# A rotary rotation split between VectorE and GpSimd, in a kernel of attention and experts

## What is computed

```
q, k, v = x @ Wq.T, x @ Wk.T, x @ Wv.T          # 32 heads of 8 features
q, k = rope(q), rope(k)                         # the rotation
kmean = mean of k over chunks of 32 tokens
gate  = q . kmean, future chunks masked, own chunk forced
allowed = 4 best chunks of each query, and causal
p = softmax(q . k / sqrt(8)) over what is allowed;  o = p @ v
o = o * rsqrt(mean(o*o) + 1e-6) * weight * sigmoid(x @ Wg1.T @ Wg2.T)
x1 = layernorm(x + o @ Wo.T)
ffn = x1 + 2 shared experts(x1) + 4 of 16 routed experts(x1), weighted
y  = layernorm(x1 + ffn)
```

```
def _rope(t):
    t1, t2 = (t[..., :D // 2], t[..., D // 2:])
    return jnp.concatenate([t1 * cos - t2 * sin, t1 * sin + t2 * cos], axis=-1)
```

## Time and profile before

| | us |
|---|---|
| median of 3 runs | 1645.65 |
| lowest, highest | 1645.09, 1646.04 |
| profiled execution, its own time | 1644.96 |
| its span | 1643.2 |
| TensorE busy | 1470.5 |
| VectorE busy | 1249.4 |
| ScalarE busy | 825.3 |
| GpSimd busy | 543.9 |

### The profile page before, as it was taken

The page is one execution under the profiler, slowest core; times in us unless marked ns, Lnnn a source line. Parts: engine busy times, 40 slices in busy tenths (PEclk is TensorE's granted clock), DMA queues, the critical chain, the costliest instruction groups (busy, mean ns, idle before and its releaser), DMA issues.

```text
span 1643.2 us, 30121 instructions
## 1 busy us (share of the span) xinstructions
PE 1470.5 (89%) x11488; PEld 789.5 (48%) x11488; DVE 1249.4 (76%) x3115; ACT 825.3 (50%) x1066; POOL 543.9 (33%) x638
## 2 busy tenths in 40 slices
PE   4688899898998989988999989989899889998597
PEld 3323465435654455534655256543565346552354
DVE  6994779768796788967787787977889677886434
ACT  4309362573627554393634836266452845349121
POOL 3204332253223532244322532234422443225032
PEclk8758899998999989998999989999899998999799
DMA  6000000000000000000000000000000000000000
GB/s 232 1 0 2 27 1 1 1 27 14 2 1 14 14 14 2 1 14 27 2 1 1 27 14 1 1 14 15 14 1 1 14 14 2 1 1 27 1 1 13
DMA packets 15623, 22.96 MB, mean 14 GB/s; under 512 B 812, under 2 KB 12758, under 8 KB 15224
## 3 DMA queue, kind: packets, MB, share of 16 engines
q1 hardware_dynamic: 15480, 21.05, 4.0%
HBM read 16.86 MB, written 4.19 MB: 13 GB/s over the span
## 4 chain that ended last, share of the span: by engine, by line
PE 66%; DVE 16%; ACT 7%; DVEq 4%; issue 3%; DMA 1%; POOL 1%; SPq 0%; POOLq 0%; ACTq 0%
PE PS L488 17%; PE PS L471 16%; PE PS L625 6%; PE PS L404 6%; ACT UQ L854 4%; PE PS L374 3%; PE PS L479 3%; PE PS L421 3%; PE PS L395 2%; DVEq L992 2%; PE PS L635 2%; DVE CM L1183 2%; ACT UK L854 1%; DMA qET<-in_w 1%; DVEq L1085 1%
## 5 line engine op out<-in xcount | busy, mean ns | idle before, releaser
L904 POOL TENSOR_TENSOR hp<-hr,hp 128x512 f16<-128x512 f32 (+1 forms) x200 | 235.3, 1177 | 673.4 <-ACT hp L741 632.2
L1183 DVE TENSOR_REDUCE CM<-PS 128x32 f32<-128x1024 f32 x320 | 385.2, 1222 | 40.5 <-PE PS L404 34.7
L488 PE MATMUL PS<-W,hp 128*128 128x256 f16 (+1 forms) x2400 | 311.5, 274 | 12.6 <-POOL hp L904 12.6
L471 PE MATMUL PS<-x1T,W 128*128 128x512 f16 (+1 forms) x1200 | 315.5, 392 | 0.8 <-ACT hr L732 0.8
L732 ACT ACTIVATE hr<-PS,CF 128x512 f32<-128x512 f32 (+1 forms) x200 | 137.5, 687 | 284.3 <-PE PS L479 255.1
L488 PEld LDWEIGHTS PS<-W,hp 128*128 128x128 f16 (+1 forms) x2400 | 215.1, 98 | 83.4 <-issue 44.3
L999 DVE TENSOR_TENSOR hr<-hr,PS 128x512 f32<-128x512 f32 x176 | 120.1, 682 | 101.3 <-ACT hr L732 98.1
L741 ACT ACTIVATE hp<-hr 128x512 f16<-128x512 f32 (+1 forms) x178 | 113.1, 635 | 162.2 <-DVE hr L999 160.6
L471 PEld LDWEIGHTS PS<-x1T,W 128*128 128x128 f16 (+1 forms) x1200 | 110.2, 100 | 113.2 <-issue 31.6
L854 ACT ACTIVATE UK<-PS 128x1024 f32<-128x1024 f32 x160 | 152.6, 1035 | 11.8 <-PE PS L421 10.8
L854 ACT ACTIVATE UQ<-PS 128x1024 f32<-128x1024 f32 x160 | 151.6, 1043 | 2.7 <-PE PS L421 0.9
(11 more groups left out here) (143 smaller groups left out, 2082.6 us busy)
## 6 DMA issues: line engine op xcount, KB each, us to landing
xT<-in_xT SPq DMA_DIRECT2D x8, 512.0 KB, 3.8
v<-in_x SPq DMA_DIRECT2D x8, 512.0 KB, 3.8
out<-x1n SPq DMA_DIRECT2D x8, 512.0 KB, 2.9
qET<-in_w SPq DMA_DIRECT2D x1, 1664.0 KB, 21.6
UK<-in_w SPq DMA_DIRECT2D x1, 1584.0 KB, 8.7
UQ<-in_w SPq DMA_DIRECT2D x1, 1584.0 KB, 11.9
kz<-in_w SPq DMA_DIRECT2D x1, 1536.0 KB, 19.8
WA<-in_wa SPq DMA_DIRECT2D x1, 776.0 KB, 5.2
```

The lines of the kernel that those rows point to most:

```text
L471: mm = pe.matmul(PS[0:w, BK_H, :], W1[:, a, k, bass.ds(f0, w)], x1T[:, e, k, :], start=(n == 0), stop=(n == 5))
L488: mm = pe.matmul(PS[:, BK_Y + j // 2, (j % 2) * D:(j % 2 + 1) * D], hp[0:w, slot, a, j * P:(j + 1) * P], W2[0:w, e, bass.ds(c, 1), :].rear ...
L904: nc.gpsimd.tensor_tensor(hp[0:w, slot, 1, :], hr[0:w, slot, :], hp[0:w, slot, 0, :], ALU.subtract).then_inc(pool_hp, 1)
L1183: nc.vector.tensor_reduce(dst, src, AX.X, ALU.max).then_inc(dve_cm, 1)
```

## The change

VectorE keeps the two products of each tile, without drains, and counts a new semaphore `dve_rot` with each. The product with the sines goes to one of two buffers `ropew`, by j % 2; before it overwrites a buffer, VectorE waits for the tile two back to be done (`pool_rope`). GpSimd does the subtraction and the addition in `turn_halves`, drains and counts `pool_rope`. TensorE and ScalarE wait for `pool_rope` where they waited for `dve_rope`. In GpSimd's order tiles 0 and 1 of the next sequence stand at the end of the turn (those of sequence 0 at the start of turn 0), tile 2 in front of the stack work of tile 0, and tile 3 in front of that of tile 1.

```
+        ropew = sb("ropew", [P, 2, 2 * D])
...
-                pe.wait_ge(dve_rope, b * NT + 2)
+                pe.wait_ge(pool_rope, b * NT + 2)
...
-                pe.wait_ge(dve_rope, (b + 1) * NT)
+                pe.wait_ge(pool_rope, (b + 1) * NT)
...
-                    act.wait_ge(dve_rope, b * NT + j + 1)
+                    act.wait_ge(pool_rope, b * NT + j + 1)
...
+            def turn_halves(b, j):
+
+                pool.wait_ge(dve_rot, 2 * (b * NT + j) + 2)
+                o = rot[:, j, :].rearrange("p (h u f) -> p h u f", h=2 * H, u=2)
+                w = ropew[:, j % 2, :].rearrange("p (h u f) -> p h u f", h=2 * H, u=2)
+                nc.gpsimd.tensor_tensor(o[:, :, 0, :], o[:, :, 0, :], w[:, :, 1, :], ALU.subtract)
+                nc.gpsimd.tensor_tensor(o[:, :, 1, :], o[:, :, 1, :], w[:, :, 0, :], ALU.add)
+                pool.drain()
+                pool.sem_inc(pool_rope, 1)
+
+            def turn(b, m, more):
+
+                if b == 0:
+                    turn_halves(0, 0)
+                    turn_halves(0, 1)
                 settled_wait(pool, pe_pv, b * NG + 2)
                 nc.gpsimd.memset(EQ[:, :, :, CR:HW].bitcast(F32), 0.0)
                 nc.gpsimd.memset(EK[:, :, :, CR + NCH:HW].bitcast(F32), 0.0)
                 for j in range(NT):
 
+                    if j < 2:
+                        turn_halves(b, j + 2)
                     nc.gpsimd.tensor_scalar(EK[:, j, :, CR:CR + NCH], ind[:, j:j + 1, :].to_broadcast([P, H, NCH]),
                                             1.0, 0.0, ALU.mult, ALU.add)
...
                 causal(NG - 1, 1)
-
-            turn(0, None)
+                if more:
+                    turn_halves(b + 1, 0)
+                    turn_halves(b + 1, 1)
...
                     dve.wait_ge(pe_proj, b * NT + j + 1)
+                    if b * NT + j >= 2:
+                        dve.wait_ge(pool_rope, b * NT + j - 1)
...
-                    w = ropeb[:, :].rearrange("p (h u f) -> p h u f", h=2 * H, u=2)
+                    w = ropew[:, j % 2, :].rearrange("p (h u f) -> p h u f", h=2 * H, u=2)
...
-                    nc.vector.tensor_tensor(w, t, sj, ALU.mult)
-                    link(nc.vector.tensor_tensor(o, t, cj, ALU.mult))
-                    nc.vector.tensor_tensor(o[:, :, 0, :], o[:, :, 0, :], w[:, :, 1, :], ALU.subtract)
-                    nc.vector.tensor_tensor(o[:, :, 1, :], o[:, :, 1, :], w[:, :, 0, :], ALU.add).then_inc(dve_rope, 1)
-                    dve.drain()
+                    nc.vector.tensor_tensor(w, t, sj, ALU.mult).then_inc(dve_rot, 1)
+                    nc.vector.tensor_tensor(o, t, cj, ALU.mult).then_inc(dve_rot, 1)
```

More of the change, by code:

```diff
@@ L199, in build @@
         pe_proj = sem("pe_proj")
-        dve_rope = sem("dve_rope")
+        dve_rot = sem("dve_rot")
+        pool_rope = sem("pool_rope")
         act_v = sem("act_v")
@@ L905, in low @@
                                         ALU.subtract).then_inc(pool_hp, 1)
-            def turn(b, m):
+            def turn_halves(b, j):
[10 more added lines that the diff above has]
+                    turn_halves(0, 1)
                 settled_wait(pool, pe_pv, b * NG + 2)
@@ L958, in turn @@
                 causal(NG - 1, 1)
-            turn(0, None)
+                if more:
+                    turn_halves(b + 1, 0)
+                    turn_halves(b + 1, 1)
+            turn(0, None, True)
             for b in range(1, B - 1):
-                turn(b, b - 1)
-            turn(B - 1, B - 2)
+                turn(b, b - 1, True)
+            turn(B - 1, B - 2, False)
             for c in range(NC):
```

## The result

| | us |
|---|---|
| changed kernel, median of 13 runs | 1657.84 |
| lowest, highest | 1650.77, 1661.81 |
| kernel before, median of the 13 runs beside them | 1648.44 |
| ratio, with its 95% interval | 1.0056 (1.0041 to 1.0071) |
| profiled execution, its own time and its span | 1661.81, 1659.2 |

The change costs 0.56%, 9.2 us of 1648.44, with an interval of 6.8 to 11.7. The kernel before stands at 1648.44 in these runs, against 1645.65 in the three runs that the forecast was made from, so the forecast of +12.6 is to be compared with +9.2. The profiled execution is the slowest of the 13, so its span is not compared with the one before; places within a seam are.

A forecast was written before the change was run, and what follows sets the result against it. TensorE was taken to bound the kernel, busy 89% of the span, so VectorE's savings count only where TensorE waits. Seven seams +9.6 and turn 0 +3 gave +12.6 us on 1645.65, so 1658; own range 1650 to 1666, chance 0.56.

The forecast's parts named there:

- The LayerNorm 0.85 us earlier: At each seam, VectorE's shorter tiles 0 and 1 let the second residual addition end at 1345.8 instead of 1346.64 us.
- The router 1.5 us earlier: At TensorE's second wait in the seam, for x1T: router starts near 1355.1 instead of 1356.60 us.
- Halves of 0.67 us: GpSimd's subtraction or addition of 256 f32 elements, from a line through 128 and 512 elements; 1.35 us per tile.
- The queue's order gives the gain back, +0.1 us at the chunk means: Tile 3's halves stand behind tile 0's stack on GpSimd, so chunk means wait until 1359.15 instead of 1359.06 us.
- behind 1360 us nothing adds to a gain: TensorE stays busy behind 1360 us, so nothing there absorbs a delay or adds to a gain.
- The routing's blocking, +1.4 us per seam: VectorE's L1052 and L1059 now meet busy GpSimd before the gate rows; bounds 0 to 2.3, seven seams sum to +9.6.
- One sign of being right: TensorE's wait before L449, the gate rows, would be over 1 us.
- Turn 0, +3 us: First gate instruction moves from 41.44 to about 47 us, +5.5; selection gets back some 2.5; bounds 1 and 6.
- Rival 1: In the routing, VectorE's two instructions meet gaps: +0.1 per seam, +1 to +3 in turn 0, 1647 to 1649; chance 0.19.
- rivals 2 and 3: GpSimd's halves: rival 2 takes 0.43 us without more blocking, 1641 us, chance 0.09; rival 3 takes 1.16 us.
- Rival 3: GpSimd's halves take 1.16 us: +2.0 at chunk means, +1.4 behind, +5 in turn 0, 1672; 0.16 together with rival 4.
- Rival 4: TensorE's fall to 1.2 GHz behind the seam's waits reaches some 3 us further: 1668 us; 0.16 together with rival 3.

The follow-up runs named there:

- e2: Changed kernel with, from turn 1 on, GpSimd's halves of tiles 2 and 3 behind the stacks of tiles 0 and 1; ratio to the kernel before 1.0076.
- e5: Changed kernel with only the halves of tiles 0 and 1 of sequences 1 to 7 on GpSimd, the rest on VectorE; ratio to before 1.0134.
- e7: Kernel before, no halves on GpSimd: VectorE makes tiles 0 and 1 as a pair, four products, one drain, four halves; ratio to before 1.0005.
- e1: Changed kernel with GpSimd doing tile 3's halves right behind tile 2's, ahead of all stack work; ratio to the kernel before 1.0039.
- e3: Changed kernel with only turn 0 undone: sequence 0's four tiles rotated wholly on VectorE with drains; ratio to the kernel before 1.0025.
- e4: Changed kernel with GpSimd waiting behind tile 3's halves for the routing's end, before low parts and the stacks of tiles 1 to 3; ratio to before 1.0165.
- e11: Kernel before with both tile pairs on VectorE; GpSimd waits for LayerNorm before tile 1's stack, for routing before first low part and tile 3's stack; ratio 0.9953.
- e12: e10 plus GpSimd waiting for the routing before tile 3's stack, with the first low part ahead of it; 1635.82 us, ratio to before 0.9938.
- e10: Changed kernel, sequence 0 on VectorE; GpSimd's order: clear stacks, halves 0 and 1, stack 0, halves 2 and 3, stacks 1 to 3; ratio to before 0.9971.

## Why the prediction was right, point by point

- **The LayerNorm 0.85 us earlier: right.** 3.35 to 2.51, 0.84. It left out a condition, that GpSimd keeps away from the LayerNorm (e2, e5, e7). In the changed kernel the very order that costs time at the chunk means fulfils it.
- **The router 1.5 us earlier: right.** In the earlier trace rows it starts 1356.60 - 1348.34 = 8.26 us behind the rank rows, after the change 1366.62 - 1359.63 = 6.99 in this seam and 6.67 to 7.03 in all.
- **Halves of 0.67 us: slightly small.** 0.72 by the median; a drain and a count add 0.18 between tiles.
- **The queue's order gives the gain back, +0.1 us at the chunk means: right.** 11.01 to 11.08. e1 shows the cause: with the order changed they come at 9.34. But the sentence that behind 1360 us nothing adds to a gain was wrong: e1's gate rows come 1.03 us earlier than before the change, and the wait for the first low part takes it back.
- **The routing's blocking, +1.4 us per seam: the mis-sized term.** From the start of the chunk means to the end of the routing it was 1366.91 - 1359.06 = 7.85 us and is 1379.53 - 1370.89 = 8.64: +0.8. L1052 and L1059 became longer by 0.49 and 0.83 us, together the 1.3 us that the prediction priced them at, but L1057, blocked before for 0.6 us, now meets the end of a short indicator instruction and takes 0.30. The working counted two more and none fewer. The gate rows moved by 0.745 us on the mean, 5.2 us in seven seams, where +9.6 was forecast; e3 puts the seams at 4.1 us. One sign of being right failed with it: the wait before the gate rows was over 1 us in two of the seven seams only (0.13 to 1.39).
- **Turn 0, +3 us: somewhat small.** The start of the selection moved by 6.0 (5.5 forecast), of which 0.85 was there before the halves: GpSimd's first wait ended at 25.10 instead of 24.25. Of the 2.5 us that the selection was to get back it got 2.0: its first tile ended at 56.19 instead of 52.19, so 4.0 are left. e3 measures 4.8 us, with some 3 us to either side. The last instruction of that tile, before and after:

```profile
51.90 0.29 DVE L1130 TENSOR_TENSOR cbias<-flag,CH 128x256 f16<-128x256 f16 x1
```
```profile
55.90 0.29 DVE L1149 TENSOR_TENSOR cbias<-flag,CH 128x256 f16<-128x256 f16 x1
```

- **The sum:** 5.2 + 4.8 = 10.0 us by these parts, 9.2 by the ratio, 12.6 forecast. Two terms erred in opposite directions. That the median, 1657.84, lies within 0.2 us of the forecast 1658 is luck: the kernel before had risen by 2.8 us meanwhile, and that made up for a forecast 3.4 us too long.
- **Rival 1** (no added blocking) fell by L1072 and L1079, and by e4, **rivals 2 and 3** by the halves' own time. (Rival 3's sum takes 3 us a seam where its terms, 2.0 and 1.4, give 3.4; nothing else rests on it.)
- **Rival 4**, the clock, fell in the form that it was given. In the first 25 us of a seam the granted clock was 0.80 five times and 0.73 twice before, and 0.80 seven times after: the fall in the seam did not grow. Nor is it the mean clock: where a run had 0.926, the changed kernel took 1660.5 to 1661.8 us (five runs) and the kernel before 1650.8 to 1652.2 (eight runs on record). What stays open is a small part. The 13 runs of the changed kernel had 0.9278 on the mean, the 18 of the kernel before beside e1 to e4 0.9294, and among runs of the kernel before 0.001 goes with about 1 us (an estimate from those at 0.926 and at 0.933), so 1.5 of the 9.2 us could lie there.

## What to carry to other kernels

An engine that gets work is a queue with an order: ask what now stands ahead of the moved work, what stands behind it, and who waits at the queue's end. Splitting a step pays only when the second engine does its part at once; here the same halves on the same engine cost 0.56% in one order and, with sequence 0 left on VectorE and GpSimd waiting for the routing, won 0.62% in another. Most of that gain needs no split at all: e11, with all halves on VectorE and the same care for GpSimd's order, won 0.47%. And keep GpSimd's SBUF work off VectorE's chains of short instructions, where five short instructions took 4.4 us instead of 0.8 (e2): let it wait for the chain, if what it owes afterwards has slack.

## What the runs showed of the hardware

- Of VectorE's instructions on SBUF, `tensor_scalar` (f32 and int32, on four elements too), `tensor_tensor`, `scalar_tensor_tensor` and the cast were held until GpSimd's instruction ended (0.17 to 0.23 us became 0.3 to 1.1, by how much of it was left). A reduction between them kept its 0.22 us, the reciprocal its 0.18 and the LayerNorm's statistics their 0.41, and the products that read PSUM took 0.68 to 0.69 us in all cases, also under GpSimd's own work. The Trainium skill ("SBUF — State Buffer", "SBUF: two separate sides") tells of an exclusive lock between VectorE's two-input or two-port instructions and GpSimd. In the changed kernel L1059, which had never met GpSimd before, took 1.06 us instead of 0.23 in all seven seams, which agrees for two inputs.
- It holds the other way round too: GpSimd's subtraction took 4.01 us instead of 0.72 behind one VectorE instruction of 3.6 us at the start.
- GpSimd's two-input instruction took 0.43 us for 128 f32 elements per partition, 0.72 for 256 in runs of four, and 1.16 for 512 in the form that subtracts an f16 tile and writes f16.
- TensorE's mean granted clock varied from run to run of one kernel (0.926 to 0.932), and with it the time by 11 us: more than the change.
- A wait of TensorE that was taken away was not a gain of its whole length (e12 against e10: 1.05 us of wait gone before the gate rows, 0.71 us of it returned as slower work at a granted clock of 0.58 instead of 0.68).
